# Layer 0's cross attention: one order of half tiles per round, score units in score banks, keys projected two chunks ahead

## The reference, cut to what matters

```python
q = (query @ Wq + bq).reshape(B, Nq, H, D).transpose(0, 2, 1, 3)      # query = layernorm(x), 128 rows
k = (key_value @ Wk + bk).reshape(B, Nkv, H, D).transpose(0, 2, 1, 3) # Nkv = 12544, H = 16, D = 16
v = (key_value @ Wv + bv).reshape(B, Nkv, H, D).transpose(0, 2, 1, 3)
attn = jnp.einsum('bhqd,bhkd->bhqk', q, k) * scale
attn = jnp.clip(attn, -CLAMP, CLAMP)
attn = jax.nn.softmax(attn, axis=-1)
x = jnp.einsum('bhqk,bhkd->bqhd', attn, v).reshape(B, Nq, Cq)
...
x = x + _L0_xattn_ref(_layernorm(x), ctx_768, ...)
x = x + _L0_attn_ref(_layernorm(x), ...)
x = x + _L0_ffn_ref(_layernorm(x), ...)   # its weights W1, W2 are first rounded to -1, 0, 1
```

## Time and profile before

| | before |
|---|---|
| median of 3 runs | 920.91 us (920.09 to 921.3) |
| the profiled execution | 919.66 us |
| its span, first to last instruction | 917.8 us |
| TensorE busy | 857.3 us, 93% of the span |
| VectorE busy | 628.9 us, 69% |
| ScalarE busy | 427.2 us, 47% |
| GpSimd busy | 217.6 us, 24% |
| mean granted TensorE clock | 0.970 |

### The profile page before, as it was taken

How to read it: one execution, slowest core, us unless ns; L and a number is a source line. 1 busy time by engine, 2 the same in 40 slices (tenths; PEclk the granted TensorE clock), 3 DMA queues, 4 the chain that set the end, 5 groups by cost and what they waited for, 6 DMA issues and landing times.

```text
span 917.8 us, 21933 instructions
## 1 busy us (share of the span) xinstructions
PE 857.3 (93%) x7662; PEld 663.3 (72%) x7662; DVE 628.9 (69%) x1104; ACT 427.2 (47%) x578; POOL 217.6 (24%) x233
## 2 busy tenths in 40 slices
PE   3889999999999999999999988998999999999798
PEld 2567777777777777777777757654688887888676
DVE  5768568568568568567567643699487878777373
ACT  2245765765765766766765721300233333333122
POOL 4182022022022022022020392350033232222000
PEclk9669999999999999999999999999999999999798
DMA  5845645645645645648635133210000000000000
GB/s 178 197 128 124 180 114 120 178 115 120 175 118 120 172 120 120 170 123 211 168 85 122 48 139 106 81 39 1 7 19 13 18 14 19 13 19 7 1 1 7
DMA packets 43867, 85.16 MB, mean 93 GB/s; under 512 B 11616, under 2 KB 26657, under 8 KB 41889
## 3 DMA queue, kind: packets, MB, share of 16 engines
q1 hardware_dynamic: 43822, 84.62, 35.9%
HBM read 45.03 MB, written 0.25 MB: 49 GB/s over the span
## 4 chain that ended last, share of the span: by engine, by line
PE 69%; issue 12%; DVE 10%; POOL 4%; ACT 2%; SPq 1%; DMA 1%; DVEq 0%; ACTq 0%; POOLq 0%
PE ps L1642 9%; PE ps L1455 9%; PE ps L1467 8%; PE ps L1373 8%; PE ps L1363 7%; PE ps L1356 6%; DVE cu L918 6%; PE ps L1650 5%; PE ps L1663 5%; PE ps L1643 2%; PE ps L1382 1%; PE ps L1389 1%; POOL ffw L510 1%; POOL wraw L508 1%; PE ps L1616 1%
## 5 line engine op out<-in xcount | busy, mean ns | idle before, releaser
L918 DVE TENSOR_REDUCE cu<-ps 128x1 f32<-128x448 f32 x448 | 250.4, 618 | 53.2 <-PE ps L1373 51.2
L668 ACT ACTIVATE pr<-ps 128x1024 f32<-128x1024 f32 x196 | 190.1, 1023 | 66.4 <-PE ps L1455 65.6
L435 POOL TENSOR_TENSOR pause<-pause 128x1 f32<-128x1 f32 x41 | 12.8, 314 | 569.5 <-DVE mr L930 377.5
L1373 PE MATMUL ps<-khl,qp 32*128 32x448 f32 x448 | 123.9, 483 | 2.6 <-DVE khl L908 0.8
L1455 PE MATMUL ps<-qs,ks 128*128 128x256 f32 x784 | 122.6, 296 | 3.3 <-ACT qs L627 3.1
L1455 PEld LDWEIGHTS ps<-qs,ks 128*128 128x128 f32 x784 | 101.9, 190 | 21.7 <-issue 20.6
L1467 PE MATMUL ps<-pr,v 128*17 128x128 f32 x3136 | 104.6, 274 | 0.5 <-DVE ps L995 0.5
L1642 PE MATMUL ps<-ks,ct 128*128 128x512 f32 x352 | 98.2, 400 | 0.3 <-ACT pr L788 0.3
L1467 PEld LDWEIGHTS ps<-pr,v 128*17 128x17 f32 x3136 | 77.2, 97 | 22.2 <-issue 19.1
L1373 PEld LDWEIGHTS ps<-khl,qp 32*128 32x128 f32 x448 | 57.9, 188 | 48.9 <-DVE cu L918 14.0
L908 DVE SCALAR_TENSOR_TENSOR khl<-ps,bk,khl 128x448 fp32r<-128x448 f32 x56 | 37.1, 682 | 74.5 <-ACT khl L615 74.5
(11 more groups left out here) (263 smaller groups left out, 1143.7 us busy)
## 6 DMA issues: line engine op xcount, KB each, us to landing
ks<-khl SPq DMA_DIRECT2D x168, 224.0 KB, 4.9
nm<-maxima SPq DMA_DIRECT2D x14, 1024.0 KB, 4.6
raw<-in_ctxT SPq DMA_DIRECT2D x14, 448.0 KB, 3.9
raw<-in_ctxT SPq DMA_DIRECT2D x28, 224.0 KB, 4.4
ffw<-in_mask_q SPq DMA_DIRECT2D x1, 1568.0 KB, 9.6
raw<-in_ctxT SPq DMA_DIRECT2D x12, 128.0 KB, 2.2
raw<-in_ctxT SPq DMA_DIRECT2D x22, 64.0 KB, 1.8
raw<-in_ctxT SPq DMA_DIRECT2D x44, 32.0 KB, 2.0
```

Of the source, the lines that this page charges most:

```text
L668: nc.scalar.activation(pr[:, (HALVES * b + u) % 4, :], bank(2 * (u % 2), 2), ACT.Exp).then_inc(S["e0_exp"], 1)
L918: V.tensor_reduce(cu2[:, h, half:half + 1], ps[:, use_bank(n), 0:NB], AX_X, ALU.max).then_inc(S["e0_red"], 1)
L1373: mm(ps[:, use_bank(n), 0:NB], qp[part, t, e, :], khl[part, 0, t, half * NB:(half + 1) * NB], start=True, stop=True).then_inc(S["e0_head"], 1)
```

## The change

The seven lists give way to one list of half tiles, `ORDER`, that is walked from round -2 to round 13 by all engines; a step is done if its chunk lies in 0 to 13.

- Each S and each W is one half tile and has its own place; halves of S and W mostly alternate.
- A unit written `u0` to `u3` goes into that score bank, one written `m` into the banks 5 to 7. 16 of the 32 units of a round are `u`. The next S on that bank waits for the unit's maximum too, and the unit waits for the exponential of the S before it.
- F and the rescaling stand at the start of a round, ahead of its first S.
- The four K steps stand near the end of round c and project chunk c + 2. Round -2 projects chunk 0, the end of round -1 chunk 1, and round 12 has no K.
- GpSimd splits the raw chunk before it spreads the maxima, in the prologue too, and ScalarE's two H steps stand apart.
- In the last round the sums of W1 and W2 are asked for after the eighth W half, not after the fourth; VectorE's reduction still follows the first S pair.
- VectorE's branch around the clipping stands at each half tile, not at each tile.

```diff
-LIST = [["K0", "F", "K1", "S", "K2", "K3", "W", "m", "m", "m", "V0", "V1", "m", "m", "V2", "V3", "m", "m"]]
-LIST += [["S", "m", "m", "m", "W", "m", "m"]] * 5
-LIST += [["W", "R0", "R1", "V4", "V5", "V6", "R2", "R3", "L", "", "", "S"]]
+ORDER = (
+    "F u1 m X V S S m m W S W V H u3 u0 u1 m m V S W H W S W m m m S W S m m S W u0 m W u3 m u2 S W "
+    "V W u0 u1 m S V m S u2 m m u3 W u1 u2 K R u0 u3 K R u1 V S V K W R W E R L K S W S "
+).split()
+EARLY_KEYS, EARLY_UNITS = 4, 0
...
+        if kind == "S":
+            later, i = divmod(n + 2, HALVES)
+            banks = (2 * (i % 2), 2 * (i % 2) + 1)
...
+        elif kind == "K":
+            later, i = divmod(n + EARLY_KEYS, 4)
+            later, banks = later + 1, (ring,)
+        elif kind == "m":
+            later, i = divmod(n + EARLY_UNITS, UNITS)
+            later, banks = later + 1, (int(word[1]),) if word[0] == "u" else (ring,)
...
+            split_lo0(1, 1)
+            pool.wait_ge(S["e0_lo"], 3)
             pool.wait_ge(S["qs_rows"], 192)
             spread_half(0, 0)
             pool.wait_ge(S["e0_dm_half"], 1)
-            split_lo0(1, 1)
-            pool.wait_ge(S["e0_lo"], 3)
...
                 for b in range(2):
+                    split_lo0(c + b, b)
+                    pool.wait_ge(S["e0_lo"], c + b + 2)
                     spread_half(c + b - 1, 1 - b)
-                    split_lo0(c + b, b)
...
+                    elif kind == "K":
+                        if i % 2 == 0 and (not isinstance(c, int) or x > 0):
+                            act.wait_ge(S[f"e0_keys{1 - xb}"], 192 * (x2 + xb))
+                            act.wait_ge(S["e0_head"], UNITS * (x - 1) + 8 * i + 16)
+                        key_block_hi(x, i)
...
-                    if c == NCH - 1 and t == 0:
+                    if c == NCH - 1 and (kind, i) == ("S", 3):
                         dve.wait_ge(S["ld_ffw"], 32)
...
+                for b in banks:
+                    user = user_before(c, at, b)
+                    if user is None or user in waited:
+                        continue
...
+                    if kind == "S":
+                        pe.wait_ge(S["e0_exp"], HALVES * x + i + 3)
...
-                if t == 1:
-                    pe.wait_ge(S["e0_red"], UNITS * NCH)
...
+                    if isinstance(c, int) and c == NCH - 1 and (kind, i) == ("W", 7):
+                        pe.wait_ge(S["e0_red"], UNITS * NCH)
```

More of the change, by code:

```diff
@@ L104 @@
-STEPS, USES = steps()
-BANKS = 3
-USED_BY = {n: (kind, i) for row in STEPS for kind, i, n in row if n is not None}
-assert USES % BANKS == 0
-def use_bank(n):
-    return 5 + n % BANKS
-def bank_of(kind, i):
-    return use_bank(next(n for n, use in USED_BY.items() if use == (kind, i)))
-def user_before(n):
-    at = n - BANKS
-    while at % USES not in USED_BY:
-        at -= BANKS
-    kind, i = USED_BY[at % USES]
-    return kind, i, at < 0
+ORDER = (
+    "F u1 m X V S S m m W S W V H u3 u0 u1 m m V S W H W S W m m m S W S m m S W u0 m W u3 m u2 S W "
+    "V W u0 u1 m S V m S u2 m m u3 W u1 u2 K R u0 u3 K R u1 V S V K W R W E R L K S W S "
+).split()
@@ new lines, with done_in, user_before @@
+STEPS = order()
+USERS = {b: [at for at, step in enumerate(STEPS) if b in step[2]] for b in (0, 1, 2, 3, 5, 6, 7)}
+def done_in(c):
+    return [(at, kind, i, banks, later) for at, (kind, i, banks, later) in enumerate(STEPS)
+            if not isinstance(c, int) or 0 <= c + later < NCH]
+def user_before(c, at, b):
+    users, back = USERS[b], 0
+    k = users.index(at)
+    while not isinstance(c, int) or c - back >= -2:
+        k -= 1
+        if k < 0:
+            k, back = len(users) - 1, back + 1
+        kind, i, _, later = STEPS[users[k]]
+        if not isinstance(c, int) or 0 <= c - back + later < NCH:
+            return kind, i, later - back
+    return None
@@ L127, in unit_of @@
+def bank_of(kind, i):
+    return next(banks[0] for k, n, banks, _ in STEPS if (k, n) == (kind, i))
 def unit_of(m):
@@ L1395, in large_sum @@
                 pe.wait_ge(S["e0_large"], c + 1)
-                mm(ps[:, use_bank(n), 0:1], ones, large[:, :], start=True, stop=True).then_inc(S["e0_flag"], 1)
-            def tile(c, b, count, t, ones=2):
-                for z in range(2):
-                    if t == 0:
-                        pe.wait_ge(S["ks_ones"], ones)
-                        pe.wait_ge(S[f"e0_keys{b}"], 192 * count)
-                        pe.wait_ge(S["e0_top"], 4 * c + 2 * z + 2)
-                    scores0(c, b, 2 * t + z)
@@ L1407, in weigh_tile @@
-            def weigh_tile(c, b, t):
-                if t == 0:
-                    pe.wait_ge(S["e0_scaled"], c + 1)
-                for z in range(2):
-                    weigh0(c, b, 2 * t + z)
-            def step0(c, b, count, t, first=False, only=None):
-                x, xb = c + 1, 1 - b
-                for kind, i, n in STEPS[t]:
-                    if kind == "S" and not first:
-                        if t < TPC - 1:
-                            tile(c, b, count, t + 1)
-                        elif only is None:
-                            tile(c + 1, 1 - b, count + b, 0)
-                    elif kind == "W" and not first:
-                        weigh_tile(c, b, t)
-                    elif kind not in "SW":
-                        prepare(x, xb, kind, i, n, first, only)
```

319 lines of the change are left out of this document (150 added, 169 removed).

## The result

The changed kernel took 955.64 us (median of four runs, 947.86 to 957.56), the kernel before 920.58 us beside it: **ratio 1.0365, 95% interval 1.032 to 1.0409, slower.** The profiled execution took 954.34 us with a span of 952.5, against 919.66 and 917.8. The forecast was 910.0, so its direction was wrong.

A forecast was written before the change was run, and what follows sets the result against it. TensorE was taken to bound the fourteen rounds. Rounds -11.3, prologue -3.6 and F to thresholds +4.0 summed to -10.9 us, for a median of 910.0 us; own range 904 to 916, with rivals 901 to 918.5.

The forecast's parts named there:

- a round after: TensorE's rounds: from 34.56 us to 33.8 after waits removed and switches added, bounds 33.0 and 34.7.
- waits taken away: In a round before: TensorE's waits for free banks and at the round's end, 3.8 us of 34.56, would go.
- switches added: In a round: TensorE changing between whole-array, 32-row and 17-column matmuls more often adds 2.7 us.
- a last one: Round 12, which has no K, would take 31.6 us.
- Rival 3: In the rounds: units holding score banks delay S and W; at a 35.3 us round, 928 us; chance 0.08.
- Rival 2: In the rounds: dearer switches or half the old waits remaining give a 34.5 us round, 918.5 us; chance 0.14.
- Waits: In a round after: waits that stay under the new order, 0.4 us, with 1.2 as upper bound.
- The first F: End of the prologue: first F at 59.0 instead of 62.64, -3.6 us, bounds -6 and +1.
- 0.2 to 5 us by the mask: Prologue: a VectorE step beside GpSimd's halving of the mask may be blocked for 0.2 to 5 us.
- F to thresholds: End of the rounds: last F to thresholds takes 11.9 us against 7.9, +4.0, bounds +3 and +5.5.
- behind the thresholds: After the thresholds: the remaining 398.7 us of the span stay as they are.
- rivals 1 and 4: Rival 1: the forecast itself, 910.0 us, chance 0.64. Rival 4: more gain, a 32.9 us round, 899 us, chance 0.14.

The follow-up runs named there:

- placed kernel: Changed kernel with 87 small zero matmuls and one wait (175 TensorE instructions) put ahead of its loop in idle time; 920.48 us, ratio 1.0027 to the kernel before.
- ring alone: Changed kernel with 87 zero matmuls ahead of its loop and all units in the three ring banks, none in score banks; 1033.83 us, ratio 1.1255.
- keys late: Changed kernel with 109 zero matmuls ahead of its loop and keys projected one chunk ahead at the round's start; 956.04 us, ratio 1.0426.
- 212 more: Changed kernel with 212 semaphore increments more on TensorE ahead of its unchanged loop; 935.12 us, one run.
- 89 more: Changed kernel with 44 zero matmuls and a wait, 89 TensorE instructions more, ahead of its loop; 965.03 us, one run.

## Why the prediction was wrong

- **The failing step is "a round after".** It summed waits taken away and switches added on the engines, and took the rest of the round for unchanged: the refetch of TensorE's loop was a term that it put at nothing. TensorE's branch at the end of each second round was in it at its old 0.2 us without being named. The change put some 44 instructions more ahead of the loop (the K of chunk 1 moved into the prologue), and 34.9 of the 40 us came from there: 22.4 in the rounds with a branch, 12.5 in those behind them, mostly by the clock. What is left of the miss, 5.5 us, is a round that is 0.4 longer than forecast, twelve times, and a last one of 32.5 for 31.6. The list of DMA queues had the row for the fetches, 21 in all and none in the loop behind its first iteration, which said that the loop was kept, though not how near the edge.
- **No rival had this mechanism.** Rival 3 ended slower, by a unit that holds a score bank; the placed kernel's rounds take 34.19 us, all but one, so it does not happen. Rival 2 put the round at 34.5.
- **The round without the pauses** is 34.19 us, not 33.8, within the bounds of 33.0 and 34.7. S to W, W to S and unit groups came as priced. Waits are 0.56, not 0.4, by TensorE's timeline of the placed kernel:

```profile
279.52 0.67 PE L1376 MATMUL ps<-khl,qp 32*128 32x448 f32 x5
280.12 0.86 PE L1366 MATMUL ps<-wv,ct 128*128 128x256 f32 x5
...
294.64 0.63 PE L1420 MATMUL ps<-pr,v 128*17 128x128 f32 x16
295.49 0.55 PE L1376 MATMUL ps<-khl,qp 32*128 32x448 f32 x2 [0.22 <-ACT pr L672]
295.96 1.28 PE L1357 MATMUL ps<-ct,wk 128*128 128x448 f32 x5
```

  A group of five units takes 0.60 (0.20 over 0.40); the units behind one W start after 0.85, not 0.56, with ScalarE named, and take 0.47. What is left, some 0.25, is known by difference alone: switches of 3.0 rather than 2.7, or old waits of under 3.8. So within a round the mechanism was right, and the gain of 0.37 us a round is half of the 0.76 forecast.
- **The waits of the old round, and who removed them.** The forecast let seven banks for units take away nearly all waits. With the ring alone the new order takes 42.7 us, with the keys late 37.5. So this order needs the banks and the early keys; how many of the old order's 3.8 us each removed, the runs do not show.
- **The first F** was +2.0, not -3.6, outside the bound of +1. The block of "0.2 to 5 us by the mask" was named, but the step to 59.0 has no term for it. It took its full size, though beside the memset and not beside the halving of the mask. Without it the placed kernel's first F is 6.7 us earlier.
- **F to thresholds** was +3.6 for +4.0 forecast, and behind the thresholds nothing changed.
- **Had the loop been well placed**, the change would have given no gain, 1.0027 (1.0002 to 1.0052): rounds of 0.37 us less, twelve times, 4.4 us, are eaten by 3.6 us at the end and a first F 3.9 us later. By that ratio the forecast of 910.0 would have been some 13 us too low (920.91 x 1.0027 = 923.4), and outside its range even so: the first F, 7.6 us later than forecast, and the rounds, 0.4 each, make up most of that.
- **A slip in the chances**: rivals 1 and 4 and half of 2 add up to 0.85, not 0.86.

## What to carry to other kernels

Before an edit to a long loop is priced, look at the instruction queue's packets inside it. If there are none, any edit that adds instructions ahead of the loop or in it may bring them, here at 3 to 5 us a branch and a lower clock behind. If time is lost with "issue" named at a loop's edge, move the loop by cheap instructions in idle time before doubting the order, and try more than one distance: here 175 and 212 more cured the changed kernel, 89 did not. Small operations of VectorE on a serial path should not meet a long GpSimd instruction: move that into idle time, or cut it.

## What the runs showed of the hardware

- A branch back of TensorE took 0.21 us or 3.3 to 4.9 us for the same loop, by its place in the stream. The clock then stood at its lower level for 6.8 us in 15 of the 19 cases and for 3.4 in the others; in the changed kernel the round behind a slow branch was 2.0 to 2.3 us longer, but for the one that held another pause.
- TensorE also paused inside rounds: 1.18 us in the changed kernel and 0.90 in the placed one, each 1.3 to 1.4 us behind the landing of an instruction packet, and up to 2.14 us with 89 more.
- A zero matmul of 64 columns took 0.057 us of TensorE (41 in 2.34), for two instructions; a semaphore increment 0.151 us for one.
- A write of 128 x 8 elements by VectorE took 0.17 us alone, 5.01 and 5.27 us beside a GpSimd memset of 6.1 us, and 0.72 us beside a quarter of it.
- Writing out the loop removes the pauses too, at 51 or 52 fetches and without a measurable cost in the kernel before (1.0019, 0.9996 to 1.0042).
